# Four 32-column tiles in place of one 128-column product, in the key, value, query and result projections of a 1444-key attention

## The reference

```python
qm = split_heads(q @ Wq.T + bq)            # 16 heads of 8
km = split_heads(k @ Wk.T + bk)            # k and v are the context: 32 x 1444 x 128
vm = split_heads(v @ Wv.T + bv)
scores = einsum('bnlh,bnph->bnlp', qm, km) / sqrt(8)
attn = softmax(where(mask, scores, -1e8), axis=-1)
out = einsum('bnlp,bnph->bnlh', attn, vm) ... @ Wo.T + bo
```

## Time and profile before

| | |
|---|---|
| runs, whole execution | 2272.82, 2285.15, 2285.22 us; median 2285.15 us |
| profiled execution | span 2267.4 us from first to last instruction; its own time is not listed apart; the runs lie 5.4 to 17.9 us above this span |
| stage B, steady part | 600 to 1690 us of the span |
| busy in that part | PE 1012.2 of 1090 us, DVE 875.1, ACT 697.1, weight loads 642.6, POOL 251.5 |
| granted TensorE clock in that part | 1.00 of full speed |

### The profile page before, as it was taken

How to read it: one execution, slowest core, us unless ns; L and a number is a source line. 1 busy time by engine, 2 the same in 40 slices (tenths; PEclk the granted TensorE clock), 3 DMA queues, 4 the chain that set the end, 5 groups by cost and what they waited for, 6 DMA issues and landing times. The chain is left out here.

```text
span 2267.4 us, 43146 instructions
## 1 busy us (share of the span) xinstructions
PE 1969.0 (87%) x16922; PEld 1258.0 (55%) x16922; DVE 1578.2 (70%) x3726; ACT 1324.7 (58%) x2169; POOL 551.4 (24%) x477
## 2 busy tenths in 40 slices
PE   3679999667999999999999999999997888888997
PEld 2546666444556556565565655556564555555554
DVE  4845666795787877878788788878771566664554
ACT  3645776683366666666666666666664555553444
POOL 1411322314122212222221222222222132311122
PEclk9879999777799999999999999999998788788999
DMA  5025554012132323233131322313222001103441
GB/s 153 1 92 183 184 173 142 4 37 91 65 109 74 126 68 118 78 105 119 68 126 63 120 85 101 121 66 122 79 89 67 16 8 16 31 1 59 67 71 40
DMA packets 120023, 189.26 MB, mean 83 GB/s; under 512 B 36770, under 2 KB 94090, under 8 KB 118414
## 3 DMA queue, kind: packets, MB, share of 16 engines
q1 hardware_dynamic: 119822, 186.50, 26.6%
HBM read 103.33 MB, written 11.76 MB: 51 GB/s over the span
## 5 line engine op out<-in xcount | busy, mean ns | idle before, releaser
L1610 DVE TENSOR_REDUCE b_part_max<-psum 128x1 f32<-128x482 f32 (+3 forms) x1248 | 737.6, 651 | 188.1 <-PE psum L1487 174.1
L1400 ACT ACTIVATE b_PT<-psum 128x800 f32<-128x800 f32 x768 | 616.6, 836 | 386.1 <-PE psum L1506 381.1
L1487 PE MATMUL psum<-b_KH,b_QBD 64*128 64x482 f32 (+1 forms) x1152 | 422.6, 445 | 45.7 <-DVE b_part_max L1610 43.3
L1506 PE MATMUL psum<-b_QS,b_KS 64*128 64x200 f32 x3072 | 438.3, 288 | 0.5 <-ACT b_PT L1400 0.3
L1506 PEld LDWEIGHTS psum<-b_QS,b_KS 64*128 64x128 f32 x3072 | 339.4, 186 | 16.2 <-issue 11.8
L1522 PE MATMUL psum<-b_PT,b_V 128*32 128x200 f32 x6144 | 341.4, 339 | 0.6 <-ACT b_PT L1400 0.6
L1487 PEld LDWEIGHTS psum<-b_KH,b_QBD 64*128 64x128 f32 x1152 | 197.3, 189 | 198.6 <-DVE b_part_max L1610 118.4
L1322 POOL TENSOR_TENSOR b_KL<-b_KF,b_KH 128x1444 fp32r<-128x1444 f32 x32 | 106.8, 3338 | 693.3 <-PE psum L1506 670.1
L1522 PEld LDWEIGHTS psum<-b_PT,b_V 128*32 128x32 f32 x6144 | 159.9, 109 | 149.1 <-ACT b_PT L1400 82.3
L1900 ACT ACTIVATE c_HE<-psum,C 128x400 f32<-128x400 f32 x128 | 75.7, 595 | 94.6 <-PE psum L2116 90.1
L1474 PE MATMUL psum<-W,b_CT 128*128 128x128 f32 (+1 forms) x768 | 117.7, 293 | 12.6 <-DVE b_part_max L1610 6.7
(11 more groups left out here) (280 smaller groups left out, 3095.2 us busy)
## 6 DMA issues: line engine op xcount, KB each, us to landing
b_KS<-b_KH SPq DMA_DIRECT2D x64, 722.0 KB
a_CT<-in_ctxt SPq DMA_DIRECT2D x32, 722.0 KB, 5.5
b_CT<-in_ctxt SPq DMA_DIRECT2D x32, 722.0 KB, 4.4
b_KS<-b_KL SPq DMA_DIRECT2D x32, 722.0 KB
a_CN<-in_ctxn SPq DMA_DIRECT2D x32, 704.0 KB
att_scratch<-b_AO SPq DMA_DIRECT2D x32, 200.0 KB, 1.9
c_G<-gates_scratch SPq DMA_DIRECT2D x4, 1600.0 KB
c_KBD<-gates_scratch SPq DMA_DIRECT2D x4, 1600.0 KB
```

Source lines behind the costliest of these rows:

```text
L1400: nc.scalar.activation(PT[:, kt % 2, 2 * a:2 * a + 2, :], psum[:, 2 * a:2 * a + 2, 0:TG], ACT.Exp).then_inc(sem["pt_ready"], 1)
L1487: m = mm(bank(b, D, size), QBD[rows, j % 2, tile * D:(tile + 1) * D], KH[rows, j % 2, at_:at_ + size], start=True, stop=True)
L1506: m = mm(bank(p, D, 2 * T, (s % 2) * 2 * T), KS[rows, j % 2, s, kt * D:(kt + 1) * D], QS[rows, j % 2, s * 2 * T:(s + 1) * 2 * T], start=Tr ...
L1610: v.tensor_reduce(part_max[0:rows, q, c:c + 1], bank(b, rows, CHUNKS[c][1]), AX.X, ALU.max)\
```

## The change

The helper `by_columns` issues a product of up to 128 result rows as up to four matmuls. Each takes 32 columns of the weights, writes 32 partitions of the same PSUM bank, and is aimed at one column strip of the array. The moving operand is the same for all four. The four kinds of jobs use it; the max jobs, the turn, the scores and `weigh` stay as they are. Semaphores, order and buffers stay too.

```diff
+            def by_columns(b, at, size, lhsT, rhs, rows=D, start=True, stop=True, shape=None):
+
+                for r in range(0, rows, 32):
+                    n = min(32, rows - r)
+                    dst = psum[r:r + n, b, at:at + size]
+                    if shape:
+                        dst = dst.rearrange("p (a c) -> p a c", a=shape[0])
+                    m = mm(dst, lhsT[:, r:r + n], rhs, start=start, stop=stop, tile_position=(0, r), skip_group_check=True)
+                return m
...
-                        m = mm(bank(b, D, size), w("xqT"), HT[:, c:c + size], start=True, stop=True)
+                        m = by_columns(b, 0, size, w("xqT"), HT[:, c:c + size])
...
-                        m = mm(bank(b, D, TG), W[:, c:c + D], HT[:, :], start=True, stop=True)
+                        m = by_columns(b, 0, TG, W[:, c:c + D], HT[:, :])
...
-                    m = mm(bank(b, D, size), w("xkT"), CT[:, j % 2, c:c + size], start=True, stop=True)
+                    m = by_columns(b, 0, size, w("xkT"), CT[:, j % 2, c:c + size])
...
-                        m = mm(bank(b, D, PAIRED // 2).rearrange("p (b t) -> p b t", b=2),
-                               K[:, K_SEL + c * D:K_SEL + (c + 1) * D], pairs[:, :, c, :], start=(c == 0), stop=(c == 1))
+                        m = by_columns(b, 0, PAIRED // 2, K[:, K_SEL + c * D:K_SEL + (c + 1) * D], pairs[:, :, c, :],
+                                       start=(c == 0), stop=(c == 1), shape=(2, T))
...
-                        m = mm(bank(b, rows, D, (k % 4) * D), CT[:, j % 2, k * D:k * D + rows], w("xvT"),
-                               start=True, stop=True)
+                        m = by_columns(b, (k % 4) * D, D, CT[:, j % 2, k * D:k * D + rows], w("xvT"), rows=rows)
```

## The result

The changed kernel takes 2242.76 us (median of four runs, 2240.0 to 2251.1) against 2285.18 for the kernel before (four runs, 2272.8 to 2285.8). The ratio on record is 0.985, with a 95% interval of 0.982 to 0.988: 1.5% faster, on the side of the forecast and within the range. The two medians alone give 0.981, just outside that interval, so the change in the whole time is known to within some 7 us. The forecast was 2248.

A forecast was written before the change was run, and what follows sets the result against it. Stage B was taken as bound by DVE's work plus its waits for PE. Value jobs 24.2, key jobs 11.4 and query pieces 1.4 make 37 us, taking the span from 2267.4 to 2230; plus 17.8, 2248 us (range 2229 to 2270).

The forecast's parts named there:

- What bounds it: Steady part of stage B: DVE's work plus its waits for PE set the time; 189.5 us of listed waits.
- the third key job: Key job right behind the turn: a drain moves ahead of it, DVE's key step comes 0.11 us later, no gain.
- The sum: Stage B: gains of value jobs, key jobs and query pieces, together 37 us.
- values: Value jobs before `weigh`: 0.22, 0.22 and 0.34 us gained in each of 31 batches, 24.2 us.
- keys: First and second key job of 30 batches: 0.19 us gained each, 11.4 us.
- queries: Last of three query pieces, one batch in four: 0.20 us gained in each of seven groups, 1.4 us.
- The longer instruction stream: About 3,500 more matmuls and as many loads on PE: cost taken as 0, with 3 us as the other end.
- The rate of four strips on one moving operand: Rounds of four matmuls in a value job: 0.109 us for 128 columns, read from `weigh` and stage C.
- The rival of longer rounds: Value and key jobs: four strips sharing one operand lengthen rounds; if doubled, 112 us more, 2397 us; chance 0.07.
- the 0.18 a round: Value jobs: about 60 cycles a matmul paid serially, time some 34 us over the median; chance 0.03.
- The drain: Before `weigh`: 0.10 us with nothing entering the array, gone in the same tiling; rival that it stays: 2267 us, chance 0.10.
- a span of 2230: Whole profiled execution: 2267.4 us before, 2230 after; 17.8 us from span to median run kept.

The follow-up runs named there:

- The two strips: The changed kernel with all four kinds of jobs in two strips of 64 columns, not four of 32: first to last `weigh` burst 1120.0 us, against 1090.5.

## Why the prediction was right

- **What bounds it.** Right. The steady part fell by 38 us with DVE's work and the clock unchanged; each wait of DVE shrank as foretold (1.12 to 1.14 said behind value jobs, 1.11 to 1.14 seen; 0.31 and 0.34; 0.66 and 0.66). For the third key job I said that its step would come 0.11 later inside its wait, with 0.40 left behind it; the wait split into 0.27 and 0.34, and the gain was nothing, as said.
- **The sum.** 37 us, measured 37.9 on the stretch. By kind: values 24.2 and 24.0, keys 11.4 and 11.6, queries 1.4 and 1.3. The query pieces' wait fell by 0.16 and not 0.20 (0.87 to 0.71). The longer instruction stream costs nothing that can be seen.
- **The rate of four strips on one moving operand.** 0.109 us a round, taken between two rows of other jobs, and 0.109 measured. The rival of longer rounds is out. So is the 0.18 a round that I had estimated from the Trainium skill (TensorEngine Tiling (Array Packing), Instruction Overhead), with about 60 cycles for each matmul paid one after the other. The Trainium skill (same title, Theoretical Speedup) lists a factor only for dimensions of at most 64. This trace agrees: four strips gain nothing in streaming, and a key job still takes 0.84 us, two rounds of 0.40 and the first load.
- **The drain.** The two strips show that the drain is a matter of neighbours with different tilings: the array drains before `weigh` for 64 columns and does not for 32. The Trainium skill (TensorEngine Tiling (Array Packing), Key Properties) says that a change of tiling mode drains TensorE. This trace agrees: it is 0.10 us before `weigh`, and 0.10 behind the turn, where the key job's start moved from 0.11 to 0.21.
- **What was off, and what was luck.** I set 17.8 us on top of a span of 2230 and got 2248; the runs came to 2242.8. Both parts were off. The span came out at 2243.2: of the 13 us more, 10 lie ahead of the first `weigh` and 3 behind the last, where the change does nothing or next to nothing. And only 1.8 us lie around a span, so the profiled execution of before was some 16 us quicker than the median run it was measured against. The two misses nearly cancel, and that 2248 lies so near 2242.8 is in part luck. What is shown is the stage's 38 us; the whole times give 34 by the ratio and 42 by the medians. The last section shows where such differences lie.

## What to carry to other kernels

When two neighbouring pieces of work on TensorE use different tilings, price the change between them (here 0.10 us of drain and the first weight load) and see whether one can take the other's tiling; it pays only where the next step of another engine waits behind that piece. A product of 128 columns in four strips streams no faster here, so all the gain lies at its ends. The strips must be issued side by side, piece by piece: strip after strip, the value jobs cost 115 us more. Before an idle slot is filled by a swap, look at who drains the bank of the piece that is moved.

## What the runs showed that was not expected

*The look-ahead over strips is short.* With eight passes of one strip issued ahead of the next strip's, the strips overlapped for about half of their work (2.08 us a job between 0.90 and 3.5). In the records of the job shown, each strip starts 0.47 us after the one before it, as that one's fifth pass of eight has begun, so no more than two strips work at once. I had expected all or nothing. The theory there said that matmuls start in the order of the program; across strips they don't, for three of `weigh` start at 1231.11 and the value job's last at 1231.22. What sets how far ahead a strip can start was not tried.

*Unchanged code moved by 10 us.* The first burst of `weigh` came at 601.8 us before and at 612.1 after. The stage's first jobs stand ahead of it too, and they are in strips now, but the delay is there already in the code that is the same. By stretch, before and after:

```profile
0.00:540.00 540.00, 412.01 (x2358) 284.68 (x2358) 347.08 (x1185) 331.13 (x696) 134.19 (x167) 0.88 0.33 104
```

```profile
0.00:550.00 550.00, 430.67 (x2358) 297.01 (x2358) 346.90 (x1183) 332.09 (x696) 132.51 (x163) 0.85 0.32 102
```

The same 2,358 matmuls took 412 us of PE's time in one and 431 in the other, at a granted clock of 0.88 and 0.85 (a mean over stretches at 1.2 and at 2.4 GHz). The other kernels' first bursts lie between 599.5 and 612.7. What decides between the levels there was not tried. It is why a stretch of the changed stage tells more than the span, and why two medians of a few runs can differ by some us from what the change does.
